# The MLP's first bias: from a matmul of TensorE into four gelu operations of ScalarE

## The reference

```python
def _forward(x, context, Wqkv, bqkv, Wos, bos, Wq, bq, Wkv, bkv, Woc, boc, W1, b1, W2, b2):
    h = _ln(x)
    qkv = (h @ Wqkv + bqkv).reshape(Bx, Nx, 3, H, D)
    ...
    x = x + (a @ Wos + bos)
    h = _ln(x)
    q = (h @ Wq + bq).reshape(Bx, Nx, H, D)
    kv = (context @ Wkv + bkv).reshape(Bx, Mx, 2, H, D)
    ...
    x = x + (a @ Woc + boc)
    h = _ln(x)
    x = x + (jax.nn.gelu(h @ W1 + b1, approximate=True) @ W2 + b2)
    return x
```

## Time and profile before

| | us |
|---|---|
| median of 3 runs | 2578.21 |
| lowest, highest | 2570.23, 2578.39 |
| the profiled execution | 2566.47 |
| its span in the trace | 2564.4 |

### The profile page before, as it was taken

One profiled execution on the slowest core, in us unless ns is written; L12 is line 12 of the kernel. 1 busy time (PEld: TensorE's weight loads), 2 busy tenths in 40 slices (PEclk: granted clock), 3 DMA queues, 4 the chain that ended last, 5 costly groups with the idle time before them and its releaser, 6 DMA issues.

```text
span 2564.4 us, 98727 instructions
## 1 busy us (share of the span) xinstructions
PE 2276.3 (89%) x37613; PEld 1919.4 (75%) x37613; DVE 1852.0 (72%) x4653; ACT 1657.8 (65%) x2884; POOL 1390.3 (54%) x3557
## 2 busy tenths in 40 slices
PE   2689888999998897999999988899999989799987
PEld 2478776788887776778887777778888877678875
DVE  3368776777777777778776777677777777677863
ACT  0256654778776664677776765477777766467775
POOL 3244334877554433688654443487755543377843
PEclk6799999999999999999999999999999999999999
DMA  6133333333333333333333333333333322333321
GB/s 153 44 91 97 89 89 93 86 94 94 99 98 89 90 88 89 91 91 92 99 98 83 101 90 90 93 86 94 91 100 97 90 79 83 87 90 89 93 76 44
DMA packets 354629, 231.55 MB, mean 90 GB/s; under 512 B 151456, under 2 KB 295584, under 8 KB 354144
## 3 DMA queue, kind: packets, MB, share of 16 engines
q1 hardware_dynamic: 349152, 222.07, 30.4%
q10 hardware_dynamic: 4128, 1.65, 0.3%
q0 software_dynamic: 864, 1.28, 0.3%
HBM read 159.87 MB, written 65.01 MB: 88 GB/s over the span
## 4 chain that ended last, share of the span: by engine, by line
PE 34%; POOL 25%; issue 21%; DMA 13%; DVE 3%; SPq 2%; POOLq 1%; ACT 1%; DVEq 0%; ACTq 0%
DMA kv_dram<-qkv_rows 6%; PE ps_scores_t L825 6%; DMA k_slots<-kv_dram 6%; PE ps_out L813 5%; PE ps_scores L788 5%; PE ps_turn L873 3%; POOL x_bias L660 3%; PE ps_wide L895 3%; POOL pre_rstd L604 2%; POOL post_rstd L604 2%; PE ps_turn L878 2%; POOL post_normed L641 2%; POOL x L644 2%; PE ps_wide L853 2%; PE ps_wide L854 2%
## 5 line engine op out<-in xcount | busy, mean ns | idle before, releaser
L1118 DVE TENSOR_REDUCE row_max<-ps_scores 128x16 f32<-128x1024 f32 x448 | 548.6, 1224 | 444.1 <-PE ps_scores L788 259.4
L727 ACT ACTIVATE probs<-ps_scores_t 128x512 f32<-128x512 f32 x896 | 535.4, 598 | 168.0 <-PE ps_scores_t L825 165.8
L1124 DVE TENSOR_TENSOR shifted<-ps_scores,row_max 128x512 f32<-128x512 f32 x896 | 611.8, 683 | 16.0 <-issue 0.6
L825 PE MATMUL ps_scores_t<-ident,shifted 128*128 128x128 f32 x3584 | 572.9, 283 | 15.9 <-ACT probs L727 15.1
L788 PE MATMUL ps_scores<-k_slots,qkv_rows 32*64 32x256 f32 x7168 | 317.4, 409 | 200.4 <-DMA k_slots<-kv_dram 150.5
L717 ACT COPY pv_sb<-ps_out 128x256 f32<-128x256 f32 x448 | 167.1, 373 | 461.0 <-PE ps_out L813 458.0
L825 PEld LDWEIGHTS ps_scores_t<-ident,shifted 128*128 128x128 f32 x3584 | 398.5, 143 | 55.4 <-issue 21.6
L813 PEld LDWEIGHTS ps_out<-probs,v_ones 128*32 128x32 f32 x14336 | 278.6, 151 | 146.9 <-issue 146.9
L813 PE MATMUL ps_out<-probs,v_ones 128*32 128x64 f32 x14336 | 343.1, 237 | 4.8 <-issue 3.7
L788 PEld LDWEIGHTS ps_scores<-k_slots,qkv_rows 32*64 32x64 f32 x7168 | 108.9, 132 | 291.7 <-issue 195.6
L707 ACT COPY qkv_rows<-ps_wide 128x384 f32<-128x384 f32 x384 | 184.3, 480 | 132.8 <-PE ps_wide L863 129.2
(11 more groups left out here) (170 smaller groups left out, 4530.9 us busy)
## 6 DMA issues: line engine op xcount, KB each, us to landing
k_slots<-kv_dram SPq DMA_DIRECT2D x448, 256.0 KB, 3.0
kv_dram<-qkv_rows SPq DMA_DIRECT2D x384, 128.0 KB, 2.2
v_ones<-kv_dram SPq DMA_DIRECT2D x896, 32.0 KB, 2.6
kv_dram<-qkv_rows SPq DMA_DIRECT2D x128, 64.0 KB, 1.7
x_in<-in_x SPq DMA_DIRECT2D x64, 64.0 KB, 1.9
ctx_in<-in_ctx SPq DMA_DIRECT2D x64, 64.0 KB, 1.9
out<-x SPq DMA_DIRECT2D x64, 64.0 KB, 1.7
kv_dram<-zeros SPq DMA_DIRECT2D x4, 512.0 KB, 7.1
```

What stands on the lines that cost most here:

```text
L727: nc.scalar.activation(probs[:, u, :, :], ps_scores_t[:, :] .rearrange("p (h t) -> p h t", h=4), ACT.Exp, scale=SCALE).then_inc(probs_read ...
L825: ins = nc.tensor.transpose(ps_scores_t[:, h * P:(h + 1) * P], shifted[:, j % 2, u, h * P:(h + 1) * P], ident[:, :])
L1118: v.tensor_reduce(row_max[:, :].rearrange("p (g n) -> p g n", n=SLOTS), ps_scores[:, :, 0:256].rearrange("p g (n k) -> p g n k", k=LEN), A ...
L1124: v.tensor_tensor(shifted[:, j % 2, u, :].rearrange("p (g n k) -> p g n k", n=SLOTS, k=LEN), ps_scores[:, 2 * u:2 * u + 2, 0:256].rearrang ...
```

## The change

The bias matmul (L892) goes. The four matmuls of a hidden layer each start their own 128 columns of `ps_wide` anew. The gelu becomes four ACTIVATEs of 128 columns, each with its column of `biases` as the bias by partition; the last one signals. `bias_parts` and its setup remain, for queries and keys.

```diff
                 def gelus(r, j):
                     act.wait_ge(hidden_ready.sem, hidden_ready.at(r, j))
-                    nc.scalar.activation(gelu[:, :, :], ps_wide[:, :].rearrange("p (c t) -> p c t", c=HCH),
-                                         GELU[layer_of(j)]).then_inc(gelu_ready.sem, 1)
+                    first = MLP[layer_of(j)] * HCH
+                    for c in range(HCH):
+                        ins = nc.scalar.activation(gelu[:, c, :], ps_wide[:, c * P:(c + 1) * P], GELU[layer_of(j)],
+                                                   bias=biases[:, first + c:first + c + 1])
+                    ins.then_inc(gelu_ready.sem, 1)
...
                     wide_read(r, j + UP + QKV)
-                    nc.tensor.matmul(ps_wide[:, :], bias_parts[:, :], bias_sel_bf[:, m * HCH:(m + 1) * HCH]
-                                     .unsqueeze(2).to_broadcast([P, HCH, P]), start=True, stop=False)
                     for c in range(HCH):
                         ins = nc.tensor.matmul(ps_wide[:, c * P:(c + 1) * P], w_1[:, m, c * P:(c + 1) * P],
-                                               turned[:, MLP_TURNED, :], start=False,
-                                               stop=c == HCH - 1)
+                                               turned[:, MLP_TURNED, :], start=True, stop=True)
                     ins.then_inc(hidden_ready.sem, 1)
```

## The result

The changed kernel took 2615.9 us in the median of 4 runs (2607.4 to 2634.3); the kernel before took 2574.4 us beside it. The ratio is 1.017, with a 95% interval of 1.011 to 1.023: some 42 us, or 1.7%, slower. The forecast was 50 us more than before, and 2628 us; the measured time is in its range (2598 to 2660). Of the 12 us by which 2628 is too high, 8 are the cost and 4 the base: the forecast started from 2578.2 us, a median of three executions.

What follows compares the result with a forecast made beforehand. The prediction took ScalarE's queue to bound the half behind each gelu; 0.59 us more per gelu, less slack, gave 25.0 + 13.3 + 8.4 + 3.6 = 50.3 us, on 2578.2 us: 2628 us, range 2598 to 2660.

Runs made afterwards that it cites:

- e6: The changed kernel with the copy of the attention output behind a gelu moved from ScalarE to VectorE; ratio to the kernel before 1.0177.
- e2: The changed kernel with its four gelus of 128 columns reading no bias, and no bias matmul; ratio to the kernel before 1.0011.
- e4: The kernel before, bias matmul kept, with two gelus of 256 columns, each with a column of zeros as bias; ratio to the kernel before 1.0017.
- e8: The changed kernel with the attention output's copy and the turned copy behind a gelu both on VectorE; ratio to the kernel before 1.0028.

## What to carry to other kernels

Before work is moved to the engine with the lower share, look for the stretch in which it lands and follow every consumer behind it in that engine's queue: here a copy and an exp, each of them something that the fuller engine waits for. Where two gates are equally late, one of them can be opened without any effect (here the exp, in e6), so a fix that does nothing does not refute the cause. Open both, or delay one alone, before deciding. A bias by partition adds some 0.09 us to a gelu that exists anyway; where it forces one operation to become four, the queue here grows by 0.52 us. And a variant that takes something else away as well, as e2 does with the matmul, is to be compared with the one that differs in one thing alone.

## What the runs showed of the hardware

- On ScalarE a column as bias adds 93 ns to the distance of two operations of 128 columns (0.266 against 0.173 us from the first to the second, 0.250 against 0.157 from there on; changed kernel and e2) and 85 ns to their duration (369 against 284 ns).
- Successive operations of ScalarE overlap by 0.10 to 0.13 us: 0.369 us long and mostly 0.250 apart, 0.284 and 0.157, 0.471 and 0.372 (e4).
- A table load does not: it starts 0.02 us after the end of the operation before (1181.49 to 1181.51 in e6), and none of the 379 of the changed kernel starts earlier. The next operation starts 0.01 us after its end. So a change of table costs 1.31 us here.
- From the end of a ScalarE operation to TensorE's weight load that waited for it, 0.12 us pass (the 1190.18 to 1190.31 above, rounded) in most cases and 0.05 in the others (96 and 31 of the 127 waits of L876 for the turned copy in the changed kernel).
- The copy of 128x256 from PSUM takes 0.37 to 0.39 us on ScalarE (the means of L701 and L717 in the kernel before and the changed one) and 0.41 to 0.42 us on VectorE (L1131 in e6, L1137 in e8).
